# Between-stage steps of a four-mixture kernel moved into tile loops: additions, normalisation, q, k, v and routing

## The chip, the cores and the metric

The kernel runs on one core of one Trainium2 chip. The metric is the device time of one execution in microseconds. Three executions of the kernel before gave 1262.35, 1270.7 and 1285.74 us, median 1270.7 us. A core has five engines that run their own instruction lists: TensorE (PE in the rows, its weight loads PEld), VectorE (DVE), ScalarE (ACT), GpSimd (POOL) and SyncE (SP), which issues most of the DMAs. They meet only at semaphores, and each engine executes its list strictly in order, so an instruction that waits holds everything behind it on its engine.

## The reference

The input `x` has B = 2 elements of 1024 rows of 128 values. Six residual stages follow one another; the first four matter here.

```python
x = x + 0.5 * L0_ffn(layernorm(x))   # stage a: top-2 of 8 experts, gelu, hidden 512
x = x + L0_attn(layernorm(x))        # stage b: causal attention, 16 heads of 8, rope on q and k
x = x + 0.5 * L0_ffn(layernorm(x))   # stage c: as a
x = x + 0.5 * L1_ffn(layernorm(x))   # stage d: top-1 of 8 experts, relu, hidden 256, biases
x = x + L1_attn(layernorm(x))        # stage e: selective scan over chunks of 64
x = x + 0.5 * L1_ffn(layernorm(x))   # stage f: as d
```

A gelu mixture takes softmax over 8 router logits per row, keeps the two largest weights, and adds `weight * expert(row)` for both. A relu mixture keeps the largest alone. Attention computes `Q, K, V = x @ W + b`, rotates Q and K, and takes causal softmax of `Q K^T / sqrt(8)`.

## The kernel before, in words

**Mixtures.** Rows are routed one batch element at a time. The router steps are tasks shared among the engines: `glogits`/`rlogits` (TensorE), `gpick`/`rpick` (VectorE chooses experts), `gcount`/`rcount` (TensorE counts), `gslots`/`rslots` (VectorE finds each row's place in an array of 128-row tiles sorted by expert). GpSimd then scatters the normalised rows to DRAM by indirect DMAs (L1604 gelu, L1629 relu; 16 or 8 per element), SyncE fetches the tiles, the tile loop computes them, SyncE stores the results in four pieces (L523, L575), and GpSimd gathers them back per row (L1611 gelu, 16 DMAs per element; L1635 relu, 8). `gadd` (L1769) and `add` (L1809) add the gathered rows into `x`.

**The gelu tile loop** (`gelu_mixture_tensor`, `_scalar`, `_vector`) has 23 tiles per element, 46 in all, and 48 iterations numbered s. TensorE in iteration s transposes tile s (L775), multiplies tile s-1 by its expert's first matrix (L784) and tile s-2 by the second (L793). ScalarE copies and applies gelu (L1189, L1194, L1199). VectorE copies the expert's first matrix of tile s into one of two buffers (L1836), which needs the multiplication of tile s-2 to be over; TensorE's L784 waits for that copy. Dictionaries that `gelu_tasks` returns say after which iteration each engine runs which extra task. Before the change VectorE does the first element's `gadd` and the next stage's statistics after the copy of s = 40, the normalisation in s = 43 and 45, and TensorE the transposes of the normalised rows (L686) in s = 44 and 46. `gadd` of the first element waits for all 16 gathers of that element. They follow its last store, which follows the first element's last tile.

**From gelu to attention.** After the loop TensorE multiplies the first element's 8 tiles of rows by the q, k, v matrix (L739), VectorE adds the biases (L1815, L1817), rotates q and k (L1464 to L1466), splits them for exact bf16 products, and SyncE transposes them by DMA. The work then runs in 8 units (element and head group). Each has 40 `s` blocks: a product on TensorE and a row maximum on VectorE (L1891, L1894). `opening` lists unit 0's s blocks and, among them, the second element's eight steps in six places: `gadd`, statistics and normalisation in two halves, transposes, q, k, v. Before, they stand after blocks 6, 10, 11, 15, 16 and 20. GpSimd (`attention_pool`) waits for both `gadd`s, clears a buffer (L1524), splits unit 1, waits until ScalarE has taken the second element's q, k, v (L1271), adds biases (L1534, L1536), rotates that element, and only then starts the units with its first causal cut (L1499), which TensorE's product with v waits for.

**From gelu to relu.** After the second gelu loop the first element is routed (`before` in `relu_tasks`), scattered and fetched. Run 0 of the relu loop has 15 tiles and runs to iteration 17; VectorE copies hidden rows of tile s-1 (L1859) and the results of tile s-3 (L1863). Then come `between`: `gadd` of the second element, its normalisation, and its routing; then run 1. GpSimd's order in this stage is fixed: scatter of element 0, gather of the gelu results of element 1, gather of the relu results of element 0, scatter of element 1, two clears (L1647), gather of element 1.

Of the kernel before, what the change touches and what calls it, by code (L numbers as in the profile page):

```python
# [20 lines left out]
D = 128  # L21
# [65 lines left out]
def build(nc, t_in, scratch, out):  # L87
    with ExitStack() as ctx:  # L88
# [245 lines left out]
        def gelu_tasks(st, nxt):  # L334
# [13 lines left out]
            vector.update({40: [t("gadd", 0), (nxt, "stats", 0)], 43: [(nxt, "norm", 0), (nxt, "stats", 1)], 45: [(nxt, "norm", 1)]})  # L348
            tensor.update({44: [(nxt, "turn", 0)], 46: [(nxt, "turn", 1)]})
            scalar.update({42: [(nxt, "stats", 0)], 44: [(nxt, "turn", 0), (nxt, "stats", 1)], 46: [(nxt, "turn", 1)]})  # L350
            return before, tensor, scalar, vector

        def relu_tasks(st, nxt):

            t = lambda w, g: (st, w, g)
            if st is relus[0]:
                before = [t(w, 0) for w in ROUTED]
                between = [(gelus[1], "gadd", 1)] + rows_of(st, 1) + [t(w, 1) for w in ROUTED]
                runs = ((0, NTL), (NTL, B * NTL))
                along = {5: [t("rweights", 0)], NTL + 5: [t("rweights", 1)]}  # L360
            else:
                before = [k for b in range(B) for k in rows_of(st, b) + [t(w, b) for w in ROUTED]]
                between = []
                runs = ((0, B * NTL),)
                along = {5: [t("rweights", 0), t("rweights", 1)]}
            along[B * NTL + 2] = [t("add", n) for n in range(HT)]
            if nxt:
                along[B * NTL + 2] += rows_of(nxt, 0)
            return before, between, runs, along
# [86 lines left out]
        def opening():  # L456

            second = {6: (0, 1), 10: (2,), 11: (3, 4), 15: (5,), 16: (6,), 20: (7,)}
            for n in range(NSB):
                yield ("s", 0, n)  # L460
                yield from [("second", 0, k) for k in second.get(n, ())]
            yield from [("returned", 0, n) for n in range(NRE)]
# [211 lines left out]
        def task_tensor(e, st, what, g):  # L674
            if what == "turn":
# [66 lines left out]
        def qkv_bank(i):  # L742

            return i % 4 + (0 if i < ST_ else 2)

        def gelu_mixture_tensor(e, st, nxt):
# [51 lines left out]
            if nxt["kind"] == "attention":  # L798
                e.wait_ge(later_in, LATER)
                for n in range(ST_):  # L800
                    qkv_tile(e, n)

        def relu_mixture_tensor(e, st, nxt):
            nf = F1 // P
            before, between, runs, along = relu_tasks(st, nxt)
# [60 lines left out]
        def unit_tensor(e, items, u, par, first):  # L866
            for what, k, n in items:
# [13 lines left out]
                elif what == "s":  # L881
                    h, group, w = s_blocks[n]
                    if n == 0:
                        e.wait_ge(AT[f"q_turned{vp}"], 16 * (v // 2 + 1))
                        e.wait_ge(AT[f"k_turned{vp}"], 16 * (v // 2 + 1))
                        if not (first and k == 0):
# [316 lines left out]
        def relu_mixture_scalar(e, st, nxt):  # L1203
            nf = F1 // P
            before, between, runs, along = relu_tasks(st, nxt)
# [452 lines left out]
        def _(e):  # L1658
# [6 lines left out]
            def task_vector(st, what, g):  # L1665
                if what in ("rpick", "rslots", "rweights", "add"):
                    return route_vector(st, what, g)
                if what in ("gpick", "gslots", "gweights", "gadd"):
                    return top_vector(st, what, g)
                blk = bass.ds(g * TPB, TPB)  # L1670
# [141 lines left out]
            def qkv_bias(i):  # L1812

                e.wait_ge(AT["qkv_done"], i + 1)
                e.tensor_tensor(qk[:, i].rearrange("p c d -> p (c d)"), ps[:, i % 4, 0:2 * D], bqkv[:, 0:2 * D],  # L1815
                                ALU.add).then_inc(AT["qkv_copied"], 1)
                e.tensor_tensor(vall[:, i, :], ps[:, i % 4, 2 * D:3 * D], bqkv[:, 2 * D:3 * D],  # L1817
                                ALU.add).then_inc(AT["qkv_copied"], 1)

            def gelu_mixture_vector(e, st, nxt):  # L1820
# [19 lines left out]
                if nxt["kind"] == "attention":  # L1840
                    e.wait_ge(later_in, LATER)
                    for n in range(ST_):
                        qkv_bias(n)

            def relu_mixture_vector(e, st, nxt):
                before, between, runs, along = relu_tasks(st, nxt)
# [262 lines left out]
```

## Time and profile before

| | |
|---|---|
| three executions | 1262.35, 1270.7, 1285.74 us |
| profiled execution | 1268.4 us, span 1266.6 us |
| granted TensorE clock, mean | 0.831 of full |
| PE busy | 924.4 us, 73% |
| PEld busy | 601.8 us, 48% |
| DVE busy | 734.8 us, 58% |
| ACT busy | 581.8 us, 46% |
| POOL busy | 572.2 us, 45% |

Stage a ends at about 151.6 us of the span; attention's first s block is at 179.5 us. The second gelu loop ends at about 660.7 us; the relu stage's last tile is at about 782.4 us. The busy shares are means over stages with different limits, so they are only the frame; what a moved step costs is read from what waits for what at its place. Times in the rows are microseconds from the start of the span; in brackets stands how long the engine was idle before the group and what released it.

### The profile page before, as it was taken

What the parts mean: (1) busy time and instruction counts of PE and PEld (TensorE: products, weight loads), DVE (VectorE), ACT (ScalarE), POOL (GpSimd) and SP (SyncE); (2) the same over time, 40 slices, a digit from 0 to 9 for tenths busy, and PEclk for the clock granted to TensorE, in tenths of its full rate; (3) what the DMA queues carried; (4) which work ended last, traced back from release to release, by engine and by line L of the source; (5) the groups of instructions that cost most, each with busy time, mean ns of one, the idle gap of its engine ahead of it and who ended that gap; (6) DMA issues with size and microseconds to landing.
All of it is one profiled execution on the core that took longest, in us unless ns stands there. A gap on an engine that the chain in (4) does not pass through costs nothing. (4 is left out here: it accounts for less than half of the span.)

```text
span 1266.6 us, 27262 instructions
## 1 busy us (share of the span) xinstructions
PE 924.4 (73%) x9728; PEld 601.8 (48%) x9728; DVE 734.8 (58%) x1936; ACT 581.8 (46%) x1238; POOL 572.2 (45%) x571
## 2 busy tenths in 40 slices
PE   2799717688889887759986646528788888874893
PEld 2699602122222222348973434216666666653572
DVE  5242667777777775424242525574788888895332
ACT  1255501456656657445552313275556666531241
POOL 1475145623333311324406262152688888881322
PEclk9999956588898879889987768666889899876897
DMA  6542131011121100032412111014111111001232
GB/s 228 156 129 67 36 63 33 1 34 34 34 35 34 34 1 1 17 131 66 115 33 77 53 48 46 11 65 139 47 41 36 40 38 39 28 20 69 60 85 71
DMA packets 118808, 72.69 MB, mean 57 GB/s; under 512 B 56332, under 2 KB 113428, under 8 KB 117783
## 3 DMA queue, kind: packets, MB, share of 16 engines
q1 hardware_dynamic: 112535, 58.36, 17.2%
q0 software_dynamic: 6144, 12.60, 3.2%
q8 instruction: 82, 1.34, 0.4%
q14 instruction: 47, 0.39, 0.1%
HBM read 37.06 MB, written 25.48 MB: 49 GB/s over the span
## 5 line engine op out<-in xcount | busy, mean ns | idle before, releaser
L1575 POOL TENSOR_TENSOR arena<-arena 128x512 f32<-128x512 f32 x126 | 214.9, 1725 | 83.0 <-ACT arena L1298 33.4
L1250 ACT ACTIVATE arena<-ps 128x1024 f32<-128x1024 f32 (+1 forms) x192 | 148.8, 810 | 94.4 <-PE ps L907 93.2
L1298 ACT ACTIVATE arena<-ps 128x512 f32<-128x512 f32 x256 | 143.4, 597 | 104.3 <-PE ps L1002 98.6
L1957 DVE TENSOR_TENSOR arena<-arena,ps 128x1024 f32<-128x1024 f32 x189 | 154.8, 860 | 18.3 <-PE ps L1015 17.2
L892 PE MATMUL ps<-arena 64*128 64x512 bf16 (+3 forms) x384 | 112.4, 391 | 57.7 <-DVE maxima L1891 23.9
L1891 DVE CUSTOM_DVE_ANT_0 arena<-ps,arena 128x512 f32<-128x512 f32 (+3 forms) x256 | 112.8, 488 | 69.0 <-PE ps L892 67.6
L1499 POOL TENSOR_SCALAR_AFFINE_SELECT arena<-arena 128x512 f32<-128x512 f32 x64 | 40.9, 639 | 202.5 <-ACT arena L1250 201.9
L1836 DVE COPY arena<-arena 128x512 f32 x92 | 48.5, 530 | 123.8 <-PE ps L784 113.4
L892 PEld LDWEIGHTS ps<-arena 64*128 64x128 bf16 x384 | 28.5, 99 | 188.3 <-DVE maxima L1891 98.7
L784 PE MATMUL ps<-arena 128*128 128x128 f32 x736 | 101.7, 283 | 11.8 <-ACT arena L1189 5.5
L793 PE MATMUL ps<-arena 128*128 x736 | 100.2, 280 | 6.0 <-ACT arena L1194 6.0
L1604 POOL DMA_INDIRECT xs_rows<-xn,gslot_of x64 | 61.9, 968 | 90.3 <-DVE gslot_of L1756 57.7
L784 PEld LDWEIGHTS ps<-arena 128*128 128x128 f32 x736 | 91.9, 196 | 16.5 <-ACT arena L1189 9.5
L922 PE MATMUL ps<-arena 128*32 128x512 f32 (+3 forms) x768 | 94.7, 570 | 5.0 <-POOL arena L1499 5.0
L793 PEld LDWEIGHTS ps<-arena 128*128 128x128 f32 x736 | 91.7, 196 | 7.7 <-issue 7.7
L907 PE MATMUL ps<-arena 64*128 64x512 bf16 (+3 forms) x384 | 89.2, 379 | 5.5 <-ACT arena L1250 5.5
L1611 POOL DMA_INDIRECT arena<-ys_rows,gslot_of x64 | 61.8, 966 | 66.8 <-DMA ys_rows<-arena 48.2
L1969 DVE TENSOR_TENSOR arena<-arena 128x1024 f32<-128x1024 f32 x63 | 77.7, 1234 | 23.5 <-ACT arena L1298 23.5
L1894 DVE TENSOR_REDUCE maxima<-ps 128x1 f32<-128x512 f32 x128 | 81.7, 685 | 13.5 <-PE ps L892 12.6
L1030 PE MATMUL ps<-arena 128*32 128x128 f32 x2048 | 83.4, 313 | 0.1
L1194 ACT ACTIVATE arena<-ps 128x512 f32<-128x512 f32 x92 | 55.2, 600 | 55.3 <-PE ps L784 55.2
L1635 POOL DMA_INDIRECT arena<-ys_rows,slot_of x32 | 30.4, 951 | 96.4 <-DMA ys_rows<-arena 87.9
(233 smaller groups left out, 1648.7 us busy)
## 6 DMA issues: line engine op xcount, KB each, us to landing
arena<-xs_rows SPq DMA_DIRECT2D x8, 512.0 KB, 5.2
ys_rows<-arena SPq DMA_DIRECT2D x8, 512.0 KB, 3.2
ys_rows<-arena SPq DMA_DIRECT2D x8, 320.0 KB, 2.5
xs_rows<-arena SPq DMA_DIRECT2D x4, 512.0 KB, 7.0
arena<-up_dram SPq DMA_DIRECT2D x4, 512.0 KB, 7.1
arena<-dn_dram SPq DMA_DIRECT2D x4, 512.0 KB, 7.8
arena<-up_dram SPq DMA_DIRECT2D x2, 1024.0 KB, 6.5
arena<-dn_dram SPq DMA_DIRECT2D x2, 1024.0 KB, 8.5
```

Of the source, the lines that this page charges most:

```text
L784: mm = e.matmul(ps[:, n1 % 2, c * P:(c + 1) * P], gwup[:, n1 % 2, c * P:(c + 1) * P], gxT[:, n1 % 2, :], start=True, stop=True)
L793: mm = e.matmul(ps[:, 4 + n2 % 2, 0:P], ghT[:, n2 % 2, c * P:(c + 1) * P], wdn[:, bass.ds(ex, 1), c, :].rearrange("p e d -> p (e d)"), sta ...
L892: mm = e.matmul(ps[:, n % 2, m * w:(m + 1) * w], qT[vp][rows, i, h // HP, :], kT[v % 3][rows, 4 * half:4 * half + w // P, h // HP, :], sta ...
L907: mm = e.matmul(ps[:, 2 + 2 * pair + h, 0:w], kT[v % 3][rows, j, pair, :], qm[rows, vp, pair, half * 512 + q0:half * 512 + 512], start=Tru ...
L922: mm = e.matmul(ps[32 * h:32 * h + 32, 6 + half, q0:512], vpad[:, vp, j, h, :], probT[:, n % 2, h, 0:w], start=(j == 0), stop=(w == P), sk ...
L1030: mm = e.matmul(ps[32 * ml:32 * ml + 32, 6 + u % 2, 0:D], cz[:, u % 2, ml, (4 * mh + t4) * 32:(4 * mh + t4 + 1) * 32], hsf[t % 3][:, m * D ...
L1250: e.activation(probT[:, m % 2, 2 * pair:2 * pair + 2, 0:w], ps[:, 2 + 2 * pair:4 + 2 * pair, 0:w], ACT.Exp, scale=SCALE).then_inc(AT["exp_ ...
L1298: e.activation(to, ps[:, 4 + n % 2, :].rearrange("p (d m t) -> p t m d", d=DBK, t=TU), ACT.Exp, scale=-1.0).then_inc(SC["decay_ready"], 1)
L1575: e.tensor_tensor(hsf[t % 3][:, cols], decayf[u % 2][:, t4 * W + cols.start:t4 * W + cols.stop], hsf[(t - 1) % 3][:, cols], ALU.mult).then ...
L1891: ins = e.tensor_tensor_reduce(masked_s[n % 2][:, m * w:(m + 1) * w], of, causal[:, 4 * P - w:4 * P], 1.0, MASKED, ALU.add, ALU.max, to)
L1894: ins = e.tensor_reduce(to, of, AX.X, ALU.max)
L1957: e.tensor_tensor(to, to, of, ALU.add).then_inc(SC["added"], 1)
```

## The change

It moves steps to other iterations and other places of the order, and changes PSUM banks and waits to fit. No arithmetic changes.

- In both gelu loops everything from `gadd` of the first element on moves six iterations earlier: from s = 40..46 to s = 34..40.
- Before attention, q, k, v of the first element become four tasks of two tiles each on TensorE in s = 42..45, their biases on VectorE in s = 43..46, through banks 6 and 7. A tile from the third on waits for the bias additions of the tile two before it.
- Before the relu stage, routing of the first element becomes tasks in s = 41..44.
- In attention's opening the second element's steps move from after blocks 6..20 to after blocks 26..36.
- In run 0 of the first relu stage `gadd` of the second element, its normalisation and transposes run beside iterations 7..13. Only its routing stays between the runs.

```diff
-            vector.update({40: [t("gadd", 0), (nxt, "stats", 0)], 43: [(nxt, "norm", 0), (nxt, "stats", 1)], 45: [(nxt, "norm", 1)]})
-            tensor.update({44: [(nxt, "turn", 0)], 46: [(nxt, "turn", 1)]})
-            scalar.update({42: [(nxt, "stats", 0)], 44: [(nxt, "turn", 0), (nxt, "stats", 1)], 46: [(nxt, "turn", 1)]})
+            vector.update({34: [t("gadd", 0), (nxt, "stats", 0)], 37: [(nxt, "norm", 0), (nxt, "stats", 1)], 39: [(nxt, "norm", 1)]})
+            tensor.update({38: [(nxt, "turn", 0)], 40: [(nxt, "turn", 1)]})
+            scalar.update({36: [(nxt, "stats", 0)], 38: [(nxt, "turn", 0), (nxt, "stats", 1)], 40: [(nxt, "turn", 1)]})
+            if nxt["kind"] == 1:
+                tensor.update({41: [(nxt, "rlogits", 0)], 43: [(nxt, "rcount", 0)]})
+                vector.update({42: [(nxt, "rpick", 0)], 44: [(nxt, "rslots", 0)]})
+            else:
+                for n in range(ST_ // 2):
+                    tensor.setdefault(42 + n, []).append((nxt, "qkv", n))
+                    vector.setdefault(43 + n, []).append((nxt, "qkv", n))
...
             if st is relus[0]:
-                before = [t(w, 0) for w in ROUTED]
-                between = [(gelus[1], "gadd", 1)] + rows_of(st, 1) + [t(w, 1) for w in ROUTED]
+                before = []
+                between = [t(w, 1) for w in ROUTED]
                 runs = ((0, NTL), (NTL, B * NTL))
                 along = {5: [t("rweights", 0)], NTL + 5: [t("rweights", 1)]}
+                tensor, scalar, vector = dict(along), dict(along), dict(along)
+                tensor.update({11: [t("turn", 2)], 13: [t("turn", 3)]})
+                scalar.update({9: [t("stats", 2)], 11: [t("turn", 2), t("stats", 3)], 13: [t("turn", 3)]})
+                vector.update({7: [(gelus[1], "gadd", 1), t("stats", 2)], 10: [t("norm", 2), t("stats", 3)], 12: [t("norm", 3)]})
...
         def opening():
-            second = {6: (0, 1), 10: (2,), 11: (3, 4), 15: (5,), 16: (6,), 20: (7,)}
+            second = {26: (0, 1), 29: (2,), 30: (3, 4), 33: (5,), 34: (6,), 36: (7,)}
...
         def qkv_tile(e, i):
-            e.wait_ge(LN["xnT_ready"], stage_of["attention"]["turn"] + i // TPB + 1)
+            e.wait_ge(LN["xnT_ready"], stage_of["attention"]["turn"] + (NTB // B if i < ST_ else NTB))
             if i == 0:
+                e.wait_ge(later_in, LATER)
+            if 2 <= i < ST_:
+                e.wait_ge(AT["qkv_copied"], 2 * (i - 1))
+            elif ST_ <= i < ST_ + 4:
+                e.wait_ge(AT["qkv_copied"], 2 * ST_)
                 e.wait_ge(GT["y_copied"], B * NTG)
-            if 4 <= i < ST_ + 4:
-                e.wait_ge(AT["qkv_copied"], 2 * min(i - 3, ST_))
...
         def qkv_bank(i):
-            return i % 4 + (0 if i < ST_ else 2)
+            return 6 + i % 2 if i < ST_ else 2 + i % 4
...
-            if nxt["kind"] == "attention":
-                e.wait_ge(later_in, LATER)
-                for n in range(ST_):
-                    qkv_tile(e, n)
```

## Rows read from the trace of the kernel before

**Rows 1.** Windows: stretch, length, busy PE, PEld, DVE, ACT, POOL; granted clock, DMA.

```profile
158.20:171.40 13.20, 0.00 (x0) 0.00 (x0) 12.44 (x29) 0.00 (x0) 10.20 (x10) 0.66 0.18 50
637.00:661.00 24.00, 20.16 (x146) 19.18 (x144) 11.94 (x48) 14.50 (x31) 0.00 (x0) 0.86 0.13 34
661.00:678.00 17.00, 7.68 (x49) 4.67 (x48) 3.69 (x18) 0.03 (x1) 7.84 (x9) 0.79 0.13 40
714.90:736.40 21.50, 9.21 (x43) 6.58 (x43) 13.00 (x60) 1.66 (x4) 7.70 (x9) 0.52 0.10 31
```

**Rows 2.** Timeline, DVE, first gelu loop: start, duration, engine, line, [idle before].

```profile
117.41 0.43 DVE L1836 COPY arena<-arena 128x512 f32 x1 [1.47 <-PE ps L784]
...
124.99 4.12 DVE L1836 COPY arena<-arena 128x512 f32 x2 [1.47 <-PE ps L784]
129.57 0.43 DVE L1836 COPY arena<-arena 128x512 f32 x1 [0.46 <-PE ps L784]
129.92 4.41 DVE L1769 SCALAR_TENSOR_TENSOR x<-arena,gweight,x 128x128 f32<-128x128 f32 x16
...
136.37 0.43 DVE L1836 COPY arena<-arena 128x512 f32 x1 [0.47 <-issue]
```

**Rows 3.** Timeline of POOL: the last gather of the first element; landing time of gathers.

```profile
123.35 0.99 POOL L1611 DMA_INDIRECT arena<-ys_rows,gslot_of  x1 [0.30 <-issue]
...
DMA to landing us min/median/max: 2.4/2.5/3.8
```

**Rows 4.** Timeline of PE: same place, then q, k, v.

```profile
136.90 1.13 PE L784 MATMUL ps<-arena 128*128 128x128 f32 x8 [2.69 <-issue]
...
152.01 5.40 PE L739 MATMUL ps<-wqkv,xnT 128*128 128x384 f32 x16 [0.45 <-ACT arena L1199]
```

**Rows 5.** Timeline of DVE: the first rotation.

```profile
158.18 0.69 DVE L1464 TENSOR_TENSOR arena<-arena 128x512 f32<-128x512 f32 x1
```

**Rows 6.** Timeline of POOL in the opening of attention.

```profile
188.91 1.80 POOL L1524 MEMSET arena<- 128x2048 f32 x1 [14.03 <-DVE x L1769]
...
211.12 4.50 POOL L1534 TENSOR_TENSOR arena<-arena,bqkv 128x2048 f32<-128x2048 f32 x1 [12.21 <-ACT arena L1271]
...
237.63 0.64 POOL L1499 TENSOR_SCALAR_AFFINE_SELECT arena<-arena 128x512 f32<-128x512 f32 x1 [2.11 <-ACT arena L1250]
```

**Rows 7.** Timeline of DVE in the opening of attention.

```profile
184.38 4.41 DVE L1769 SCALAR_TENSOR_TENSOR x<-arena,gweight,x 128x128 f32<-128x128 f32 x16
...
213.35 11.14 DVE L1894 TENSOR_REDUCE maxima<-ps 128x1 f32<-128x512 f32 x16
```

**Rows 8.** Costliest groups of the page: count, busy us, mean ns of one, idle before.

```profile
L1250 ACT ACTIVATE arena<-ps 128x1024 f32<-128x1024 f32 (+1 forms) x192 | 148.8, 810 | 94.4 <-PE ps L907 93.2
```

**Rows 9.** Timeline of POOL, DVE and PE in the second gelu loop.

```profile
631.09 0.94 POOL L1611 DMA_INDIRECT arena<-ys_rows,gslot_of  x1 [0.30 <-issue]
...
637.36 4.41 DVE L1769 SCALAR_TENSOR_TENSOR x<-arena,gweight,x 128x128 f32<-128x128 f32 x16
...
643.80 0.43 DVE L1836 COPY arena<-arena 128x512 f32 x1 [0.47 <-issue]
...
644.33 2.04 PE L784 MATMUL ps<-arena 128*128 128x128 f32 x8 [2.68 <-issue]
```

**Rows 10.** Timeline after that loop: routing of the first element on PE, scatter on POOL.

```profile
660.57 1.90 PE L716 MATMUL ps<-rw,xnT 128*128 128x8 f32 x16
...
667.63 1.00 POOL L1629 DMA_INDIRECT xs_rows<-xn,slot_of  x1 [35.60 <-DVE slot_of L1794]
```

**Rows 11.** Timeline of POOL and DVE in the first relu run, and behind it.

```profile
696.65 0.94 POOL L1611 DMA_INDIRECT arena<-ys_rows,gslot_of  x1 [0.30 <-issue]
...
697.75 0.29 DVE L1863 COPY arena<-ps 128x128 f32<-128x128 f32 x1 [0.59 <-PE ps L860]
...
716.92 0.94 POOL L1635 DMA_INDIRECT arena<-ys_rows,slot_of  x1 [19.33 <-DMA ys_rows<-arena]
...
736.36 1.00 POOL L1629 DMA_INDIRECT xs_rows<-xn,slot_of  x1 [9.64 <-DVE slot_of L1794]
```

More of the change, by code:

```diff
@@ L364, in relu_tasks @@
                 runs = ((0, B * NTL),)
[L365 to L369, printed above, removed]
+                tensor, scalar, vector = [{5: [t("rweights", 0), t("rweights", 1)]} for _ in range(3)]
+            for engine in (tensor, scalar, vector):
+                engine[B * NTL + 2] = [t("add", n) for n in range(HT)] + (rows_of(nxt, 0) if nxt else [])
+            return before, between, runs, tensor, scalar, vector
         AT = {k: sem(f"att_{k}") for k in (
@@ L674, in task_tensor @@
         def task_tensor(e, st, what, g):
-            if what == "turn":
+            if what == "qkv":
+                for i in (2 * g, 2 * g + 1):
+                    qkv_tile(e, i)
+            elif what == "turn":
                 n = st["turn"] + g
@@ L797, in gelu_mixture_tensor @@
                     task_tensor(e, *task)
-            if nxt["kind"] == "attention":
-                e.wait_ge(later_in, LATER)
-                for n in range(ST_):
-                    qkv_tile(e, n)
         def relu_mixture_tensor(e, st, nxt):
             nf = F1 // P
-            before, between, runs, along = relu_tasks(st, nxt)
+            before, between, runs, along, _, _ = relu_tasks(st, nxt)
             for task in before:
@@ L885, in unit_tensor @@
                         e.wait_ge(AT[f"k_turned{vp}"], 16 * (v // 2 + 1))
-                        if not (first and k == 0):
+                        if first and k == 0:
+                            e.wait_ge(GT["y_copied"], B * NTG)
+                        else:
                             e.wait_ge(AT["returned_copied"], NRE * v)
@@ L1204, in relu_mixture_scalar @@
             nf = F1 // P
-            before, between, runs, along = relu_tasks(st, nxt)
+            before, between, runs, _, along, _ = relu_tasks(st, nxt)
             for task in before:
@@ L1669, in task_vector @@
                     return top_vector(st, what, g)
+                if what == "qkv":
+                    if g == 0:
+                        e.wait_ge(later_in, LATER)
+                    qkv_bias(2 * g)
+                    return qkv_bias(2 * g + 1)
                 blk = bass.ds(g * TPB, TPB)
@@ L1839, in gelu_mixture_vector @@
                         task_vector(*task)
[L1840 to L1843, printed above, removed]
             def relu_mixture_vector(e, st, nxt):
-                before, between, runs, along = relu_tasks(st, nxt)
+                before, between, runs, _, _, along = relu_tasks(st, nxt)
                 for task in before:
```

4 lines of the change are left out of this document (2 added, 2 removed).

## The prediction

> **What bounds the kernel now.** The chain of waits ends in the last stage and says nothing of the places touched, so I read the stages by windows, and the timeline at each moved step. The kernel is a sequence: no stage's work overlaps the next one's much, so a delay of the last engine to finish a stage goes into the end in full. The reader is to see three holes in the windows [rows 1]: TensorE works 0.00 us in the 13.2 us of the first rotation while VectorE works 12.44; 7.68 in the 17 us after the second gelu loop; 9.21 in the 21.5 us between the relu runs. The change aims at these. The gelu loop between them is different. A tile takes (124.99 - 117.41)/4 = 1.895 us [rows 2], and TensorE sets that: VectorE copies for 0.43 us and then sits idle for 1.47 until L784 frees a buffer. So VectorE has room there, but no more than two buffers' worth of delay.
>
> **First gelu loop: `gadd` six iterations earlier.** The copy before `gadd` is that of s = 40, at 129.57, so s = 34 is the copy at 117.41 [rows 2]. `gadd` needs all 16 gathers. GpSimd starts the last at 123.35; the relu stages' gathers, of the same form, land 2.5 us after their start (median) [rows 3], so it lands at 125.9. At s = 40 that was past and cost nothing. At s = 34 VectorE stands from 117.8 to 125.9, and the copies of s = 35 and on stand behind it. Gathers and stores don't move: they follow tile 22. From the start of `gadd` to the next copy takes 136.37 - 129.92 = 6.45 us [rows 2], so the copy of s = 35 is at 132.35 and not at 119.31, 13.0 late. How much reaches TensorE? Before, the copy of s = 41 was 4.9 us late (136.37 against 129.57 + 1.9), and TensorE stood 2.69 [rows 2, 4]: the buffers swallow 2.2. So it will stand 10.8 us where it stood 2.69: **+8.1**.
>
> Two smaller terms. Two copies took 4.12 us together where two take 0.86 alone, beside GpSimd's clearing of buffers, and the copy of s = 40 was 0.8 late for it [rows 2]. In the new order VectorE is in the wait or in `gadd` then: **-0.8**. [...] No row shows `gadd` beside a memset; if it were locked out as the copies were, 2 to 3 us would be added.
>
> [...] After 10.8 us of standing I expect it: **+1.6** (0 to 3). [...]
>
> **First gelu loop: q, k, v inside.** They are 5.40 us of TensorE [rows 4] in a loop that TensorE bounds, so they lengthen it: **+5.4**. The bias additions run beside it. Last matmul of the loop: 151.6 + 8.1 - 0.8 + 1.6 + 5.4 = 165.9. VectorE leaves earlier: behind the last pair come only s = 46 and half of s = 47, some 2.8 us at 1.895 each. So the last pair ends at 163.1; from the last q, k, v matmul (157.41) to the rotation (158.18) it took 0.8 [rows 4, 5]. Rotation at 163.9 against 158.18: **+5.7**. What was gained by taking the 5.4 us off the path is less than the new wait. The transposes by DMA and the first s block follow the rotation unchanged.
>
> **Attention's opening.** VectorE and TensorE do the same steps at other places, which costs them nothing by itself. `gadd` of the second element stood at 184.38 [rows 7]; after the longer loop its gathers land some 14 us later than before, and after block 26 it is past them. But GpSimd's prologue hangs on these steps. It waited 14.03 us for `gadd` and 12.21 for q, k, v, began the biases at 211.12, and was done 2.11 us before the first cut at 237.63: 24.4 us of its own work [rows 6]. q, k, v now stand 16 blocks later, at 11.14/16 = 0.70 us each [rows 7] 11.1 us. So: biases at 211.1 + 5.7 + 11.1 = 227.9, done at 252.3; the cut is wanted at 237.63 + 5.7 = 243.3. It is 9.0 late, and behind it stand the product with v on TensorE, and behind that, in order, unit 1's s blocks. ScalarE can do the next step's two exponentials meanwhile, 2 x 0.81 [rows 8], so I give 2 back: **+7.0** (bounds 0, if something else holds the cut as long, and 9). GpSimd's split for unit 1 is 18 us later too, but had some 35 us to spare.
>
> **Second gelu loop.** s = 40 is the copy before 637.36; the last gather starts at 631.09 and lands at 633.6 [rows 9]. s = 34 is six tiles earlier, at 625.6. The copy of s = 35 comes at 633.6 + 6.4 = 640.1. TensorE resumes at 640.6 in s = 36 where it resumed at 644.33 in s = 42. The same work to the last transpose, then five more full iterations with 1.9 us of router logits [rows 10] and 0.7 of counts: loop end at 640.6 + 16.2 + 9.5 + 2.6 + 2.0 = 670.9, 10 us later than 660.6. [...] Routing, though, is now done by s = 44: counts after the last transpose (656.1) plus 3.8 + 1.9 + 2.6 = 664.4, slots 2.9 later, 667.3. The scatter began at 667.63 [rows 10]. **0** (-3 to +3): what routing inside the loop gains, the wait for the gather takes. Scatter, fetch and the second element's gather then keep their times; stores of the last tiles come 8 us before that gather.
>
> **First relu run.** The last gather of the second element starts at 696.65 and lands at 699.2; VectorE reaches iteration 7's end at 698.0 [rows 11]: a wait of 1.2. Then it does in the loop what it did between: of the 13.00 us that it worked there, 3.69 are routing (what it did in the window after the second gelu loop, 18 instructions), so 9.3 [rows 1]. With that a table load on ScalarE and two transposes of 0.6 on TensorE. This loop is a ring of short steps with VectorE in it, so I take nearly all: 1.2 + 9.3 + 2.7 (an estimate: 1.3 to 1.5 on ScalarE and 1.2 on TensorE), less 1 of slack: run 0 is 12 us longer (8 to 17). Between the runs only routing is left. But GpSimd gathers the first element's results before it scatters the second's: it started that at 716.92, 8 DMAs to 726.7, and then sat idle 9.64 us to 736.36 [rows 11]. That idle time is all that can be gained. **+2.5** (-1.5 to +7.5). Run 1 and all behind it are unchanged.
>
> **Sum** against the profiled execution's 1268.4 (span 1266.6): 5.7 + 7.0 + 0 + 2.5 = 15.2, 1283.6 us, 1.2% more. The profiled execution is 2.3 below the median of 1270.7, inside the spread of the three. Two per cent, about what a measurement of this kernel tells from no change, is 25 us, so this forecast is "no difference", on the slow side.
>
> **Rivals.** *The prologue is harmless* (0.20): the cut is not what unit 0 waits for, or the loss is made up over the units. For it: GpSimd is idle for most of attention. Against: order is fixed on each engine. 5.7 + 0 to 2.5: 1275. *Faster, all moves hidden* (0.06): the gathers are in time for s = 34, and what is put into the loops costs nothing. Gains: 6.6 from the loop's last matmul to the rotation, about 10 of the 17 us after the second loop, 9.6 of GpSimd's idle time: 1242. It decides only if the gathers land 8 us sooner, and nothing in the change moves them. *Slower by over 2%: the clock stays down* (0.10): after 10.8 us of standing TensorE stays at half clock to each loop's end. Eight matmuls then take 2.04 for 1.13 [rows 4, 9], 1.8 us more per tile, 11 tiles: 20 in each loop and 5.4 more for q, k, v, less the 1.6 counted, 42 us above the forecast, 1325. It decides above six slow tiles per loop. For it: the fall after 2.68 us. [...] The forecast has 0.60; 0.04 are left for unforeseen costs of either sign.
>
> **Numbers.** The forecast's own range is 1276 to 1292 (POOL 0 to 9, relu -1.5 to 7.5, not all at one end). The range 1266 to 1298 adds the harmless prologue and part of the slow side. Faster by over 2%: 0.05; within: 0.82; slower: 0.13, the clock and the upper tail.
>
> **What would show it.** VectorE idle about 8 us before `gadd` in both gelu loops, released by the gathers; TensorE idle near 11 us after it, in s = 36; eight matmuls at about 2 us behind it; rotation near 164; first cut near 252 with GpSimd busy just before it and ScalarE long done; first relu scatter near 15 us (12.7 from attention) later than 667.6; scatter of the second element straight behind GpSimd's gather, without the 9.64 us. I am wrong if `gadd` at s = 34 shows no wait, if GpSimd is idle before the first cut, or if run 0 of the relu loop grows by less than 8 us.

## The result: 1.8% slower, with most of it lost between the first gelu loop and attention

| | before | after |
|---|---|---|
| median (executions) | 1271.89 us (4, 1262.35 to 1285.74) | 1293.06 us (4, 1290.70 to 1294.42) |
| profiled execution, span | 1268.4, 1266.6 us | 1294.15, 1292.3 us |
| granted TensorE clock, mean | 0.831 | 0.817 |

The ratio is 1.0185, 95% interval 1.0132 to 1.0237: slower, but whether by more or less than the 2% set as the bound is open, since the interval holds 2%. Ratios, here and below, are taken over the fast runs of each kernel alone, and so are not the quotients of the medians. The forecast was 1283.6 in a range of 1266 to 1298. The busy times on the page moved little (PE, PEld, DVE, ACT and POOL had 924.4, 601.8, 734.8, 581.8 and 572.2 us before):

```profile
PE 935.3 (72%) x9728; PEld 606.5 (47%) x9728; DVE 730.1 (56%) x1936; ACT 582.6 (45%) x1238; POOL 571.0 (44%) x571
```

PE's busy time grew by 10.9 us and the others' by less or not at all, so most of the 25.7 us of span are waits. To place them, divide both spans at events that each kernel has: the start of the first element's last gather, the first rotation, the first and the last causal cut of attention, and so on. The last four columns are runs on one chip, described below.

| stretch, us | before | after | before_again | gadd_at_30 | best_38 | no_first_loop |
|---|---|---|---|---|---|---|
| start to last gather, first gelu loop | 123.3 | 124.2 | 122.8 | 123.9 | 125.7 | 124.6 |
| to the first rotation | 34.8 | 40.5 | 34.8 | 49.6 | 38.0 | 34.8 |
| to the first causal cut | 79.4 | 89.6 | 79.9 | 90.3 | 80.1 | 80.0 |
| to the last cut | 288.9 | 292.8 | 288.9 | 293.6 | 277.0 | 278.8 |
| to last gather, second gelu loop | 104.6 | 105.3 | 105.2 | 105.4 | 105.5 | 104.9 |
| to the first relu scatter | 36.5 | 35.6 | 34.2 | 43.2 | 33.6 | 35.2 |
| to the second relu scatter | 68.7 | 69.4 | 68.0 | 70.0 | 68.9 | 70.0 |
| to the last relu gather | 57.1 | 57.1 | 58.6 | 57.1 | 57.2 | 57.1 |
| to the end | 473.1 | 477.8 | 477.0 | 479.6 | 479.7 | 476.9 |

**First gelu loop.** VectorE in the kernel after (timeline; start, duration, engine, line, idle before and releaser), to be laid beside [rows 2]:

```profile
118.29 0.43 DVE L1855 COPY arena<-arena 128x512 f32 x1 [1.47 <-PE ps L800]
126.79 4.45 DVE L1788 SCALAR_TENSOR_TENSOR x<-arena,gweight,x 128x128 f32<-128x128 f32 x16 [8.08 <-DMA arena<-ys_rows,gslot_of]
...
133.28 0.43 DVE L1855 COPY arena<-arena 128x512 f32 x1 [0.47 <-issue]
...
164.72 0.69 DVE L1478 TENSOR_TENSOR arena<-arena 128x512 f32<-128x512 f32 x1
```

And TensorE, beside [rows 4]:

```profile
133.81 2.05 PE L800 MATMUL ps<-arena 128*128 128x128 f32 x8 [10.88 <-issue]
135.65 1.92 PE L809 MATMUL ps<-arena 128*128 x8
...
140.58 1.06 PE L800 MATMUL ps<-arena 128*128 128x128 f32 x8
...
162.50 1.46 PE L755 MATMUL ps<-wqkv,xnT 128*128 128x384 f32 x4
164.69 2.10 PE L809 MATMUL ps<-arena 128*128 x16
```

The copy of s = 34 is at 118.29, `gadd` behind it stands 8.08 us for the gathers, TensorE stands 10.88 us, comes back at half clock (eight matmuls in 2.05 us) and is at full again at 140.58 (1.06). Four pairs of q, k, v lie in the loop.

**Opening.** GpSimd of the kernel after, beside [rows 6], then ScalarE (of the kernel before, then of the kernel after), then TensorE of the kernel after:

```profile
210.17 1.80 POOL L1538 MEMSET arena<- 128x2048 f32 x1 [20.91 <-DVE x L1788]
229.97 4.49 POOL L1548 TENSOR_TENSOR arena<-arena,bqkv 128x2048 f32<-128x2048 f32 x1 [9.82 <-ACT arena L1285]
254.32 0.64 POOL L1513 TENSOR_SCALAR_AFFINE_SELECT arena<-arena 128x512 f32<-128x512 f32 x1
```

```profile
235.62 3.35 ACT L1250 ACTIVATE arena<-ps 128x1024 f32<-128x1024 f32 x4
```

```profile
245.18 1.94 ACT L1264 ACTIVATE arena<-ps 128x1024 f32<-128x1024 f32 x2
252.68 1.51 ACT L1264 ACTIVATE arena<-ps 128x768 f32<-128x768 f32 x2 [5.56 <-POOLq L1481]
```

```profile
255.01 1.94 PE L936 MATMUL ps<-arena 128*32 128x512 f32 x8 [6.91 <-POOL arena L1513]
```

Before, the cut had 2.11 us of idle time ahead of it; now it has none, and TensorE's product with v waits 6.91 us for it. The ScalarE rows are the ones to look at twice. Before, the first four exponentials ran on without a stop (3.35 us). Now ScalarE stands 5.56 us after two, until GpSimd reports its rotation done (L1481). GpSimd is not only late with the cut, it holds ScalarE too.

**Second gelu loop and relu run.** VectorE, then TensorE, then GpSimd, beside [rows 9, 10, 11]:

```profile
654.91 4.41 DVE L1788 SCALAR_TENSOR_TENSOR x<-arena,gweight,x 128x128 f32<-128x128 f32 x16 [7.40 <-DMA arena<-ys_rows,gslot_of]
...
720.45 4.41 DVE L1788 SCALAR_TENSOR_TENSOR x<-arena,gweight,x 128x128 f32<-128x128 f32 x16 [3.19 <-DMA arena<-ys_rows,gslot_of]
```

```profile
661.90 2.05 PE L800 MATMUL ps<-arena 128*128 128x128 f32 x8 [10.19 <-issue]
```

```profile
687.99 1.00 POOL L1643 DMA_INDIRECT xs_rows<-xn,slot_of  x1 [34.68 <-DVE slot_of L1813]
...
747.38 0.94 POOL L1649 DMA_INDIRECT arena<-ys_rows,slot_of  x1 [29.42 <-DMA ys_rows<-arena]
...
757.36 1.00 POOL L1643 DMA_INDIRECT xs_rows<-xn,slot_of  x1 [0.30 <-issue]
```

Both additions in a loop wait for their gathers. From scatter to relu gather it is 59.4 us against 49.3 before: run 0 (the relu loop over the first element's tiles) is 10.1 longer. The second scatter follows the gather at once (0.30) where GpSimd sat idle 9.64 us, so only 0.6 of it is left in the time between the two scatters.

### The profile page after: what moved, and what is told of

The parts are those of the page before. It is cut to its first block and busy times, and to the rows that moved or that the text cites. A ratio compares the mean times of both kernels' runs of the same rounds, so it can differ in the third digit from the quotient of the medians.

```text
span 1292.3 us, 27264 instructions
## 1 busy us (share of the span) xinstructions
PE 935.3 (72%) x9728; PEld 606.5 (47%) x9728; DVE 730.1 (56%) x1936; ACT 582.6 (45%) x1238; POOL 571.0 (44%) x571
## 5 line engine op out<-in xcount | busy, mean ns | idle before, releaser
L1906 DVE CUSTOM_DVE_ANT_0 arena<-ps,arena 128x512 f32<-128x512 f32 (+3 forms) x256 | 113.0, 488 | 70.6 <-PE ps L906 68.9
L1855 DVE COPY arena<-arena 128x512 f32 x92 | 42.7, 464 | 119.9 <-PE ps L800 108.0
L936 PE MATMUL ps<-arena 128*32 128x512 f32 (+3 forms) x768 | 98.3, 590 | 11.4 <-POOL arena L1513 11.3
L1625 POOL DMA_INDIRECT arena<-ys_rows,gslot_of x64 | 60.8, 950 | 82.7 <-DMA ys_rows<-arena 64.1
L1044 PE MATMUL ps<-arena 128*32 128x128 f32 x2048 | 86.0, 320 | 0.1
```

What stands on the lines that cost most here:

```text
L936: mm = e.matmul(ps[32 * h:32 * h + 32, 6 + half, q0:512], vpad[:, vp, j, h, :], probT[:, n % 2, h, 0:w], start=(j == 0), stop=(w == P), sk ...
L1044: mm = e.matmul(ps[32 * ml:32 * ml + 32, 6 + u % 2, 0:D], cz[:, u % 2, ml, (4 * mh + t4) * 32:(4 * mh + t4 + 1) * 32], hsf[t % 3][:, m * D ...
L1906: ins = e.tensor_tensor_reduce(masked_s[n % 2][:, m * w:(m + 1) * w], of, causal[:, 4 * P - w:4 * P], 1.0, MASKED, ALU.add, ALU.max, to)
```

## The experiments

The first eight ran on another chip than the last four. There the kernel before takes 86 to 91 us more, in the stretches with tile loops and in the last stage: engines stand many microseconds at a time with a releaser that the profile calls remote. It was not traced there itself; relu_run_only, which is the same up to the relu stage, shows the first gelu loop's stretch to the rotation at 51.0 us for 34.8, while first rotation to first cut (79.8) and attention (288.8) are as on the other. Whether this is the chip or something else that differed between the two sets of runs is not shown; "that chip" and "the slower chip" stand for it below. Rows of VectorE of the changed kernel on that chip (timeline, second gelu loop):

```profile
648.90 0.43 DVE L1855 COPY arena<-arena 128x512 f32 x1 [13.06 <-remote]
...
697.27 0.43 DVE L1855 COPY arena<-arena 128x512 f32 x1 [10.95 <-remote]
...
706.79 4.41 DVE L1788 SCALAR_TENSOR_TENSOR x<-arena,gweight,x 128x128 f32<-128x128 f32 x16
```

The last row is what makes this chip useful: the loop is slower, the gathers are in time for s = 34, and `gadd` shows no wait, in the first loop neither (at 151.50). The wait is taken away with no edit of the kernel, though the chip's own stands come in its place.

| on that chip | median us | ratio, 95% | last gather to rotation | rotation to cut | cut to last cut | gather to 1st relu scatter | to 2nd scatter |
|---|---|---|---|---|---|---|---|
| second_only | 1372.4 | 1.0121 (1.0077 to 1.0165) | 51.3 | 88.3 | 291.0 | 54.7 | 80.1 |
| first_loop_only | 1362.37 | 1.0035 (0.9990 to 1.0079) | 51.4 | 81.4 | 289.2 | 53.8 | 80.3 |
| second_loop_only | 1354.69 | 0.9976 (0.9932 to 1.0020) | 51.4 | 80.2 | 288.9 | 44.3 | 86.6 |
| relu_run_only | 1351.02 | 0.9978 (0.9942 to 1.0015) | 51.0 | 79.8 | 288.8 | 54.0 | 80.3 |
| after_again | 1366.64 | 1.0021 (0.9977 to 1.0065) | 50.2 | 90.2 | 293.6 | 45.1 | 85.4 |
| second_back | 1357.6 | 0.9963 (0.9928 to 0.9999) | 50.2 | 81.3 | 291.6 | 45.5 | 85.5 |
| pool_swap | 1373.1 | 1.0053 (0.9996 to 1.0109) | 49.6 | 90.6 | 293.5 | 44.3 | 80.2 |
| gadd_at_38 | 1363.09 | 1.0027 (0.9991 to 1.0064) | 50.7 | 88.9 | 290.3 | 51.8 | 79.4 |

The first four were compared with one set of runs of the kernel before (median 1355.58), the next four with another (1361.24).

### The four parts alone

**second_only**: the kernel before with the second element's steps at the changed places of the opening.

```diff
-            second = {6: (0, 1), 10: (2,), 11: (3, 4), 15: (5,), 16: (6,), 20: (7,)}
+            second = {26: (0, 1), 29: (2,), 30: (3, 4), 33: (5,), 34: (6,), 36: (7,)}
```

> The kernel before with one edit: in attention's opening the second element's steps stand after blocks 26 to 36 and not 6 to 20. Theory (GpSimd's prologue holds unit 0): q, k, v of the second element are done 11 us later, GpSimd starts the biases near 222, ends its rotation near 246.5, the first cut is near 247 where it was 237.6, and the time grows by 9 to 11 us (ratio 1.007 to 1.009). Rival (prologue harmless, the loss is in the gelu loops): first cut at most 2 us later than at the end of the opening, ratio 1.000. Either way the first s block stays near 179.5.

Measured: 1.0121, 16 us. The cut is 88.3 us after the rotation instead of 79.8. GpSimd:

```profile
256.59 4.49 POOL L1534 TENSOR_TENSOR arena<-arena,bqkv 128x2048 f32<-128x2048 f32 x1 [9.94 <-ACT arena L1271]
...
280.95 0.64 POOL L1499 TENSOR_SCALAR_AFFINE_SELECT arena<-arena 128x512 f32<-128x512 f32 x1
```

Again no idle time before the cut, and ScalarE stands the same 5.56 us before its third exponential. The stretches show 8.4 us up to the cut and 2.2 in attention behind it; the interval reaches from 10 to 22 us, so these two may be all of it.

**first_loop_only**: the kernel before with the change's first gelu loop.

```diff
-            vector.update({40: [t("gadd", 0), ...
+            o = 0 if nxt["kind"] == "attention" else 6
+            vector.update({34 + o: [t("gadd", 0), ...
```

> The changed kernel's first gelu loop (addition at s = 34, q, k, v in the loop) with everything else as before, the opening's steps after blocks 6 to 20 too. Theory: VectorE waits 8 us for the gather, TensorE stands 10.9, rotation is at 164 (5.7 later); the second element's gather lands some 2 to 3 us after block 6 would ask for it, so the first cut is 6 to 9 us later than before; ratio 1.005 to 1.007. Rival (the opening is what costs, the loop's wait is bought back by q, k, v off the path): rotation within 1 us of 158, ratio 1.000.

Measured: 1.0035, no difference that the interval can tell from none; the stretch to the rotation is 51.4 against 51.0. The 8 us of wait that were expected did not come, so this says what the move costs without them: nothing that can be told from none, and no gain either. The first cut comes 1.6 us later after the rotation (81.4 for 79.8), where 6 to 9 in all were expected.

**second_loop_only**: the same with the offset the other way round, and routing in the loop.

> The kernel before with only the second gelu loop changed: addition at s = 34 and the first element's routing in s = 41 to 44; first loop, opening and the steps between the relu runs as before. Theory (wait and gain cancel): VectorE waits 7 to 8 us for the gather, first relu scatter within 1.5 us of where it stood after the last gather (36.5 us after the last gather's start), ratio 0.999 to 1.001. Rival (routing inside the loop is a true gain): scatter 5 us or more earlier, ratio 0.995. Rival (the wait costs): scatter 5 us later, ratio 1.004.

Measured: 0.9976. Without a wait the first scatter comes 9.7 us sooner (44.3 for 54.0), which on the first chip was 0.9 only. But 6.3 of it is lost by the second scatter (86.6 for 80.3). The rival "a true gain" is right about the scatter on this chip and not about the time.

**relu_run_only**: the second element's addition, normalisation and transposes beside run 0.

> The kernel before with only run 0 of the first relu stage changed: second element's addition, normalisation and transposes beside iterations 7 to 13, its routing alone between the runs. Theory (GpSimd's queue binds): run 0 is 10 us longer, GpSimd goes from the first element's gather to the second's scatter without the 9.6 us of idle time, and that scatter starts 0 to 2 us later than before relative to the first scatter (68.7 us); ratio 1.000 to 1.0015. Rival (the gap is saved): scatter 5 us or more earlier, ratio 0.995.

Measured: 0.9978 (0.9942 to 1.0015), scatter to scatter 80.3, as in second_only and first_loop_only, which lack this part. The relu gather starts 70.3 us after the first scatter where it started 60.8 in first_loop_only, and GpSimd's idle time before the second scatter falls from 9.65 to 0.30: it takes up the longer run.

### Undoing one part, and two other orders

**after_again**: the changed kernel on that chip, for the four beside it.

> The changed kernel again, on the chip of the runs below. On the chip of the four runs before, the tile loops themselves stood still for 7 to 17 us at a time with nothing of the kernel to wait for, so the gathers were in time for s = 34. Theory (the parts add up): where the loops run clean the ratio is 1.013 to 1.024 as first measured; where they stand, VectorE shows no wait before the two additions and the ratio is the product of the four parts measured there, 1.011 (1.004 to 1.018). Rival (the parts interact): on such a chip 1.018 or more.

Measured: 1.0021 (0.9977 to 1.0065), where the first comparison had 1.0185 (1.0132 to 1.0237). The opening costs as much here (90.2 for 79.8). What differs is that the loops gain: 0.8 in the first and 8.9 in the second, where the first chip lost 5.7 and gained 0.9. The expected product of the four parts, 1.011, was missed, on the fast side; each part has an interval of some 0.004 to both sides, so that is no proof that they help each other.

**second_back**: the changed kernel with the `second` line of before.

> The changed kernel with the opening's steps back after blocks 6 to 20. Theory (ScalarE's third exponential and the first cut wait for GpSimd's rotation): first cut comes 80 to 84 us after VectorE's first rotation and not 89.6, ScalarE does not wait for GpSimd, the rest of attention is 2 to 4 us shorter; 8 to 14 us faster than the changed kernel, ratio to before 1.005 to 1.010. Rival (the loss is in the gelu loops and the clock): equal to the changed kernel within 3 us.

Measured: 0.9963 (0.9928 to 0.9999), 0.0058 or some 8 us below after_again, though the two intervals overlap. The cut, 8.9 us sooner after the rotation, has its idle time back:

```profile
245.04 4.51 POOL L1548 TENSOR_TENSOR arena<-arena,bqkv 128x2048 f32<-128x2048 f32 x1 [12.97 <-ACT arena L1285]
...
271.57 0.64 POOL L1513 TENSOR_SCALAR_AFFINE_SELECT arena<-arena 128x512 f32<-128x512 f32 x1 [2.11 <-ACT arena L1264]
```

**pool_swap**: GpSimd scatters the second element before it gathers the first element's relu results.

```diff
                     gelu_gather(1, 1)
-                    relu_gather(0, 0)
                 relu_scatter(st, 1)
                 if st is relus[0]:
+                    relu_gather(0, 0)
```

> The changed kernel with one edit in GpSimd's order in the first relu stage: the second element's scatter stands before the gather of the first element's results. Theory (GpSimd's queue kept the shortened gap from showing): the scatter starts right behind its slots, 5 to 6 us sooner than in the changed kernel, and run 1 with it; 4 to 6 us faster than the changed kernel. Rival (the gather is then late for the additions after run 1, or stores bind the fetch): no difference.

Measured: 1.0053 (0.9996 to 1.0109), no gain where 4 to 6 us less than the changed kernel were expected. The second scatter is 5.2 us sooner (80.2 for 85.4), and the stretch behind it 10.0 longer (68.1 for 58.1). GpSimd and VectorE in run 1, first of pool_swap, then of after_again:

```profile
839.27 13.78 POOL L1661 MEMSET arena<- 128x16384 bf16 x1
...
842.70 10.38 DVE L1819 TENSOR_SCALAR wtop<-wtop 128x8 f32<-128x8 f32 x1
```

```profile
836.87 13.77 POOL L1661 MEMSET arena<- 128x16384 bf16 x1
...
848.70 1.97 DVE L1819 TENSOR_SCALAR wtop<-wtop 128x8 f32<-128x8 f32 x1
```

GpSimd clears two buffers in a row here; the rows show the second clear, of 13.8 us. An operation of VectorE on 8 values per partition starts inside it and takes 10.38 us, to the clear's end (853.05, against 853.08), and the tile copies stand behind it. The same operation takes 0.17 us in the kernel before, where no clear lies beside it (L1800 at 695.34). In after_again it starts 1.9 us before the clear's end and takes 1.97. Both times it ends within 0.03 us of the clear's end (850.67 against 850.64 in after_again); by what mechanism is not shown. So the swap, which put the gather between the scatter and the clears, let this operation start 8.4 us further ahead of their end. That is most of the 10.0 us; the rest stays open.

**gadd_at_38**: `gadd` after s = 38 in both loops, what hangs on it four iterations later.

```diff
-            vector.update({34: [t("gadd", 0), ...
+            vector.update({38: [t("gadd", 0), ...
```

> The changed kernel with the additions four iterations later in both gelu loops (s = 38, all that follows four later, q, k, v in s = 45 to 47, routing in s = 45 and 46). Where the loops run clean, theory (the wait is the loss): no wait of VectorE before the addition, TensorE stands under 4 us there and not 10.9, rotation 6 to 8 us sooner than in the changed kernel, first relu scatter 1 to 3 us sooner after the last gather; 7 to 10 us faster than the changed kernel. Rival (the wait is bought back, work moved early is worth as much): within 3 us. Where the loops stand still: no wait in either, and this kernel 0 to 4 us slower than the changed one, because less is hidden.

Measured: 1.0027, beside 1.0021 of the changed kernel. No wait was there to be saved on this chip; the second loop gives 6.7 of its gain back (51.8 for 45.1), and the second scatter comes 6.1 sooner after it (79.4). In after_again, second_back and second_loop_only, the kernels here with an early first scatter and GpSimd's old order, 5 to 6 us are lost again before the second. The traces narrow this down. In first_loop_only ScalarE comes back from a remote stand of 8.48 us 32.7 us after the first scatter, with four tiles of the relu run already copied. In second_loop_only it comes back from one of 29.52 us at 34.2, with the run's first tile. So the earlier scatter did not move the end of the stand, and fewer tiles lay ahead of it; what ends it is not known.

### The dose of the wait, and two attempts at something better

These four ran on a chip on which the kernel before takes 1269.79 us (23 executions, 1258.54 to 1279.60), as in the first comparison.

> The kernel before, unchanged, for a trace on the same chip as the three beside it. If this chip is like the one of the first comparison, VectorE reaches the copy of s = 34 near 117 us, the first cut starts near 238 and the span is 1265 to 1275. If it is like the one of the earlier experiments, the span is 1340 to 1375, engines stand 7 to 17 us at a time in both gelu loops with a remote releaser also in this kernel, the rotation is near 190 and the first cut 79 to 81 us behind it, and from the first relu scatter to the last relu gather of that stage it takes 128 to 129 us.

**before_again** is the kernel before: 1271.37 us, span 1269.5, cut at 237.57. Its stretches show how far two traces of one kernel differ: 0.0 to 2.3 up to the last relu gather, and 3.8 in the last stretch. Against it the changed kernel has 22.8 us more span, not 25.7.

**gadd_at_30**: the changed kernel, `gadd` four iterations earlier still.

```diff
-            vector.update({34: [t("gadd", 0), (nxt, "stats", 0)], 37: ...
+            vector.update({30: [t("gadd", 0), (nxt, "stats", 0)], 37: ...
```

> The changed kernel with gadd of the first element after the copy of s = 30 instead of 34 in both gelu loops; all else stays. The dose of the disputed wait. Theory (gadd waits for gathers that do not move, and all but what the two buffers swallow reaches TensorE): on the first kind of chip VectorE reaches s = 30 four tiles, 7.6 us, earlier and stands about 15 to 16 us before gadd instead of 8.1; TensorE still restarts at the same moment but with four more tiles ahead of it, so rotation is 7 to 9 us later than in the changed kernel, and the second loop the same: span 15 us longer, near 1308. On the second kind of chip, where gadd at s = 34 found its rows, gadd at 30 waits up to 10 us or nothing. Rival (TensorE stood in the changed kernel for another reason, instruction supply or the clock): the wait appears on VectorE, but rotation moves by less than 3 us.

Measured, in one execution: 1314.49 us, span 20.3 above the changed kernel, where 15 were expected. VectorE in both loops, and TensorE in the first:

```profile
126.47 4.44 DVE L1788 SCALAR_TENSOR_TENSOR x<-arena,gweight,x 128x128 f32<-128x128 f32 x16 [15.55 <-DMA arena<-ys_rows,gslot_of]
...
665.27 4.41 DVE L1788 SCALAR_TENSOR_TENSOR x<-arena,gweight,x 128x128 f32<-128x128 f32 x16 [15.04 <-DMA arena<-ys_rows,gslot_of]
```

```profile
133.84 2.05 PE L800 MATMUL ps<-arena 128*128 128x128 f32 x8 [18.71 <-issue]
```

The wait grows by 7.5 and 7.6 us, the stretches by 9.1 (49.6 for 40.5) and 7.5 (43.2 for 35.6). TensorE restarts at the same moment, 133.84 for 133.81, with four more tiles ahead. The rival that something else had held it (below 3 us) is out.

**best_38**: gadd_at_38 with the `second` line of before.

> The changed kernel with two edits: gadd of the first element after the copy of s = 38 in both gelu loops (normalisation, transposes, q, k, v and routing four iterations later with it), and the second element's steps in attention's opening back after blocks 6 to 20. Theory: the two costs of the change are gone and its gains stay. On the first kind of chip: no VectorE wait before gadd in either loop (last landing 125.9, gadd at s = 38 would come near 125 to 127), rotation at 157 to 160 against 158.2 before, first cut at 236 to 240, first relu scatter 3 to 8 us earlier than before, relu run as changed, 0 to +2: span 0 to 8 us under before, ratio 0.994 to 1.000. On the second kind: ratio 0.993 to 1.000. Rival (q, k, v and routing inside the loops cost as much as they gain, whatever the wait): ratio 1.000 to 1.006.

Measured: 1266.54 us, 0.9992 (0.9953 to 1.0032). Half of the theory held: the first cut is again 80.1 us after the rotation. The rotation was expected at 157 to 160 and came at 163.7, 5.5 us later than before. 2.3 of that lie ahead of the last gather; 3.2 lie between it and the rotation. VectorE and TensorE there:

```profile
126.02 4.44 DVE L1855 COPY arena<-arena 128x512 f32 x1 [1.47 <-PE ps L800]
130.38 4.43 DVE L1788 SCALAR_TENSOR_TENSOR x<-arena,gweight,x 128x128 f32<-128x128 f32 x16
```

```profile
130.56 1.13 PE L800 MATMUL ps<-arena 128*128 128x128 f32 x8 [1.80 <-issue]
...
137.39 2.03 PE L800 MATMUL ps<-arena 128*128 128x128 f32 x8 [4.69 <-issue]
```

`gadd` has no wait, but the copy ahead of it takes 4.44 us beside GpSimd's clears (from 126.60 on), and the two together make TensorE stand 1.80 and 4.69. So of the changed kernel's 5.7, the later place gets back 2.5.

**no_first_loop**: the kernel before with the change's second gelu loop and relu run.

> The kernel before with the change's second gelu loop (gadd at s = 34, routing in the loop) and its first relu run alone; first gelu loop and opening stay as before. Theory: each of the two was within noise alone (0.9976 and 0.9978), so together 0.993 to 1.001; rotation and first cut as before, first relu scatter 0 to 3 us earlier than before on the first kind of chip and 5 to 10 on the second, where the gathered rows are in time. Rival (the opening was the whole cost of the change and the first loop is free): this kernel and best_38 are then alike within 0.3%; if the first loop carries a cost of its own, this one is the faster by 5 us.

Measured: 1268.88 us, 0.9992 (0.9952 to 1.0033). First loop and opening are as before (34.8, 80.0); the second loop, where `gadd` waits 7.48, gains nothing (the scatter comes after 35.2, between the 34.2 and 36.5 of the two traces of before), and the relu run costs 1.2 to 1.9. Neither kernel beats the one before. The expectation took two equal times for a free first loop. They are equal, but the first loop of best_38 is not free: its trace loses 3.2 us there, and wins 1.6 and 1.1 on this one in the stretches up to the two relu scatters.

## Why the prediction was right, and by how much each step was off

The changed kernel landed in the range and on the side forecast, 9.5 us above the number. The forecast's sum was 15.2; the medians say 21.2, the spans 25.7 and, against before_again, 22.8. The range held although the opening and attention behind it came out 7.1 us above the forecast together.

**First gelu loop, +5.7: right, with its mechanism.** The wait was 8.08 for 8.1, TensorE stood 10.88 for 10.8, the stretch to the rotation grew by 5.7. The clock was at half after both long stands (eight matmuls in 2.05 us after 10.88 and after 10.19, granted clock 0.50 in the 3 us behind each). The +1.6, which the forecast adds after 10.8 us of standing for such a fall of the clock, was an estimate, and no run shows it apart from the rest; what the traces show is the way from TensorE's restart to the first transposes of the normalised rows, two iterations on: 8.87 us in the changed kernel (133.81 to 142.68) and 7.14 in the kernel before (136.90 to 144.04, eight matmuls in 1.13). In the second loop of the kernel before, the same two numbers stand for a restart at half clock and, in before_again, one at full. The open question, whether `gadd` suffers beside a clear, is answered too: GpSimd clears from 125.18 to 129.51, and `gadd` beside it takes 4.45 us where it took 4.41. gadd_at_30 shows the same cost growing with the wait, and the slower chip shows it gone where the gathers are in time (50.2 for 51.0).

**Opening, +7.0: the direction right, the size not.** It is 10.2 (89.6 for 79.4). Two terms make the 3.2. q, k, v came 12.3 us later after the rotation (229.97 - 164.72 against 211.12 - 158.18), not 11.1; 2.11 of idle time taken off, that is 10.2 us of lateness, where I had 9.0. The term that failed is the next: "ScalarE can do the next step's two exponentials meanwhile, 2 x 0.81 [rows 8], so I give 2 back". It cannot. The third exponential of unit 0 writes to memory that the second element's q and k share, so it waits for GpSimd's rotation of that element; the code has that wait (`rotated`), and the trace the 5.56 us. Had 2 us been given back, it would show behind the cut, and it does not: the third cut follows the first by 5.46 us, where it was 5.33. second_only and second_back show the cost up to the cut both ways, by 8.4 and 8.9 us of stretch. *The prologue is harmless* is refuted by the same two.

**Attention behind it, forecast 0: +3.9.** The code between the first and the last cut is the same, and the engines' work in it too. Windows of that stretch in before_again, in the kernel after and in no_first_loop (length; busy PE, PEld, DVE, ACT, POOL; granted clock, DMA share, GB/s):

```profile
237.60:526.50 288.90, 243.72 (x1693) 73.92 (x1693) 202.64 (x674) 176.83 (x243) 84.29 (x172) 0.84 0.12 23
```

```profile
254.30:547.10 292.80, 246.92 (x1689) 73.45 (x1689) 201.26 (x666) 175.77 (x241) 84.31 (x174) 0.82 0.12 23
```

```profile
239.50:518.20 278.70, 230.92 (x1693) 70.25 (x1693) 201.83 (x674) 176.10 (x243) 84.27 (x172) 0.91 0.13 24
```

VectorE, ScalarE and GpSimd do the same; PE's busy time and the length go with the clock: 288.9 us at 0.84 (before, before_again), 292.8 and 293.6 at 0.82 and 0.81, 278.7 and 277.0 at 0.91. Most of the 3.9 can be placed. From the first to the 57th of the 64 cuts the two kernels differ by 0.8 us (254.05, 254.82). The other 3.1 lie in the last seven, of the kernel before, then of the kernel after:

```profile
491.68:526.52 34.84, 26.69 (x195) 11.61 (x195) 15.83 (x62) 24.55 (x34) 4.76 (x8) 0.85 0.00 1
```

```profile
509.14:547.08 37.94, 29.51 (x195) 11.40 (x195) 15.95 (x62) 24.87 (x34) 4.76 (x7) 0.74 0.00 1
```

best_38, with the early opening, also has 0.74 and 37.58 us there, so these 3.1 are not the opening's. The 0.8 may be: on the slower chip the four kernels with the late opening take 255.5 to 256.1 us up to the 57th cut and the four with the early one 254.0 to 255.0. That the time goes with the clock is shown; what sets the clock there is not. It need not be the kernel: single executions of the kernel before on the chip of the last four runs lie between 1258.54 us with a mean clock of 0.846 and 1279.60 with 0.822.

**Second gelu loop, 0: right.** -0.9 against the first trace, +1.4 against the second. The 2.3 us between those two traces of one kernel are mostly the clock: in before_again it did not fall at this place.

```profile
644.41 1.13 PE L784 MATMUL ps<-arena 128*128 128x128 f32 x8 [2.68 <-issue]
```

From here to the router logits it is 14.5 us in before_again, and 16.2, the term of the forecast, in the first trace, where the fall is already in it [rows 9, 10]. TensorE's restart in the changed kernel is 9.5 us after the last gather's start, as worked out, and what routing in the loop gains the wait takes: on the slower chip, with no wait, the same edit gives 8.6 to 9.7.

**First relu run, +2.5: +0.6 or +1.3.** Run 0 is 10.1 us longer for 12, the wait before `gadd` 3.19 for 1.2, and GpSimd's idle time took the rest, as said.

**The rest.** Of the first comparison's 25.7, 4.7 are in the last stretch and 0.9 before the loop. The last stretch was 473.1 in the first trace of before and 476.9 to 479.7 in the five others of such a chip, so that is the luck of one trace, and it makes the profiled difference larger than the medians'.

**The other rivals.** *The clock stays down*: no, it was full again 6.8 us after the restart (granted clock 1.00 from 140.6 to 146.0 us). *Faster, all moves hidden*: its condition, gathers in time for s = 34, came true on the slower chip, and the changed kernel took 1.0021 there. Even with the opening put back (second_back) it gained 0.4% and not the 2% that the rival added up: the first loop gained 0.8, and of the 8.6 that the second loop gained, 5.2 were gone by the second relu scatter.

## What to carry to other kernels

Here a step moved forward into a loop was worth something only from the moment its data had landed; find that moment in the queue that feeds it before counting any gain, and remember that it stayed put here while the loop around it may be quicker or slower. Before giving time back because an engine "can do something else meanwhile", read what that engine's next instructions wait for: here it was the same late engine. And where an idle gap of GpSimd is removed, look at what its next long clear then lies beside.

## What the runs showed of the hardware

- One program, two chips, 1270 us on one and 1356 to 1361 on the other, and the ratio of the change went from 1.0185 to 1.0021. On the slower one engines stand with a remote releaser, in the tile loops among other places, up to 13.1 us at a time on VectorE and 29.5 on ScalarE:

```profile
DVE arena L1855 <- remote: 55.0, 6, 13.1
```

  This row is from the table of waits of after_again (waiter and releaser; us in total, times, longest). In the six traces of the other kind of chip no engine has such a stand of over 1 us. What is remote could not be seen.
- The granted clock over attention lay between 0.81 and 0.91 in kernels with the same code there, and that stretch between 293.6 and 277.0 us, a difference of 16.6, more than any part of the change was worth. no_first_loop runs level with before_again up to the 17th cut (72.87 and 72.84 us from the first) and is 10.2 us ahead by the 57th (243.92, 254.08). So a single trace of a kernel does not tell what the kernel is worth there.
- TensorE kept its full clock over a stand of 1.80 us (eight matmuls in 1.13) and had half after 4.69 (2.03), in one loop of best_38. After 2.68 us at one and the same instruction it had half in one trace of the kernel before (2.04) and full in the other (1.13).
- Beside clears of GpSimd, VectorE's 128x512 copy took 4.44 us for 0.43 (best_38) and an operation on 8 values 10.38 for 0.17 (pool_swap), while the 16 operations of `gadd` took 4.45 for 4.41 (the changed kernel).
